# Maxima of a query tile over five even blocks of 462 columns in place of four of 512 and one of 256

## The reference, cut to what matters

```
def layer(x):                      # x: 2 x 48 x 48 x 192
    q, k, v = split_heads(group_norm(x) @ qkv_w + qkv_b)          # 24 x 2304 x 16 each
    attn = (q * 16 ** -0.5) @ k.T + rel_h[..., :, None] + rel_w[..., None, :]   # 2304 x 2304 a head
    attn = softmax(attn, axis=-1)
    return x + join_heads(attn @ v) @ proj_w + proj_b
```

## Time and profile before

| | before |
|---|---|
| median of three runs | 6808.28 us |
| span of the profiled execution | 6801.4 us |
| TensorE busy | 6725.5 us (99%) |
| VectorE busy | 5454.7 us (80%) |
| ScalarE busy | 4753.7 us (70%) |
| max matmuls (L805), 8640 | 3404.1 us, 395 ns each |
| max reductions (L683), 8640 | 5088.7 us, 632 ns each |
| granted clock of TensorE, mean | 0.996 |

### The profile page before, as it was taken

One profiled execution on the slowest core, in us unless ns is written; L12 is line 12 of the kernel. 1 busy time (PEld: TensorE's weight loads), 2 busy tenths in 40 slices (PEclk: granted clock), 3 DMA queues, 4 the chain that ended last, 5 costly groups with the idle time before them and its releaser, 6 DMA issues.

```text
span 6801.4 us, 139326 instructions
## 1 busy us (share of the span) xinstructions
PE 6725.5 (99%) x53600; PEld 4245.8 (62%) x53600; DVE 5454.7 (80%) x9973; ACT 4753.7 (70%) x10225; POOL 938.1 (14%) x967
## 2 busy tenths in 40 slices
PE   7999999999999999999999999999999999999998
PEld 5666666666666666666665666666666666666664
DVE  7887888778887788877888778887888878888883
ACT  3776776767767777677776767767676676767775
POOL 2111010211112110121111210102101121101110
PEclk8999999999999999999999999999999999999999
DMA  6676676767677677667676766767677676777673
GB/s 164 148 156 152 137 160 138 163 151 142 152 144 168 144 143 156 149 158 149 142 155 149 158 143 143 161 145 166 140 144 157 147 165 138 143 152 156 144 154 88
DMA packets 306307, 1013.72 MB, mean 149 GB/s; under 512 B 107440, under 2 KB 196976, under 8 KB 215920
## 3 DMA queue, kind: packets, MB, share of 16 engines
q1 hardware_dynamic: 305648, 1004.81, 68.9%
HBM read 745.26 MB, written 255.69 MB: 147 GB/s over the span
## 4 chain that ended last, share of the span: by engine, by line
PE 96%; DMA 1%; DVE 1%; issue 0%; ACT 0%; SPq 0%; POOL 0%; DVEq 0%; ACTq 0%
PE work L805 30%; PE work L878 27%; PE work L796 27%; PE work L824 7%; PE work L843 3%; PE work L862 2%; PE work L851 1%; DMA moving<-rel_scratch 1%; DVE mpart L683 1%; PE work L830 0%; DVE xb L674 0%; ACT probs L561 0%; DMA back<-attention_scratch 0%; DVE hi L721 0%; PE work L835 0%
## 5 line engine op out<-in xcount | busy, mean ns | idle before, releaser
L683 DVE TENSOR_REDUCE mpart<-work 128x1 f32<-128x512 f32 (+1 forms) x8640 | 5088.7, 632 | 1079.7 <-PE work L805 1013.1
L561 ACT ACTIVATE probs<-work 128x512 f32<-128x512 f32 (+1 forms) x8640 | 4100.2, 564 | 866.6 <-PE work L796 852.1
L805 PE MATMUL work<-mkeys,hi 128*128 128x512 f32 (+1 forms) x8640 | 3404.1, 395 | 10.6 <-DVE mpart L683 8.8
L796 PE MATMUL work<-moving,keys 113*128 113x512 f32 (+1 forms) x8640 | 3299.9, 383 | 10.9 <-DMA moving<-rel_scratch 5.7
L805 PEld LDWEIGHTS work<-mkeys,hi 128*128 128x128 f32 x8640 | 1643.6, 190 | 622.4 <-DVE mpart L683 324.0
L878 PE MATMUL work<-probs,vall 128*17 128x288 f32 x27648 | 2013.1, 409 | 0.0
L796 PEld LDWEIGHTS work<-moving,keys 113*128 113x128 f32 x8640 | 1642.1, 190 | 362.3 <-ACT probs L561 39.2
L878 PEld LDWEIGHTS work<-probs,vall 128*17 128x17 f32 x27648 | 637.3, 96 | 846.8 <-ACT probs L561 358.3
L824 PEld LDWEIGHTS work<-image,tab 128*48 128x48 f32 x6912 | 401.6, 124 | 544.9 <-ACT probs L561 513.2
L490 POOL TENSOR_TENSOR full<-full,hi 128x384 f32<-128x384 f32 x576 | 583.5, 1016 | 938.7 <-DVE hi L721 937.6
L495 POOL TENSOR_TENSOR rden<-oraw,rden 128x576 f32<-128x576 f32 x96 | 137.1, 1428 | 3955.3 <-DMA rden<-inverse_scratch 3955.3
(11 more groups left out here) (42 smaller groups left out, 646.8 us busy)
## 6 DMA issues: line engine op xcount, KB each, us to landing
moving<-rel_scratch SPq DMA_DIRECT2D x1728, 144.0 KB
moving<-qk_scratch SPq DMA_DIRECT2D x288, 576.0 KB
rel_scratch<-hi SPq DMA_DIRECT2D x192, 432.0 KB, 5.7
rel_scratch<-full SPq DMA_DIRECT2D x192, 432.0 KB, 5.5
moving<-rel_scratch SPq DMA_DIRECT2D x288, 288.0 KB
image<-qk_scratch SPq DMA_DIRECT2D x384, 144.0 KB, 3.2
keys<-qk_scratch SPq DMA_DIRECT2D x192, 288.0 KB, 7.8
qk_scratch<-split_hi SPq DMA_DIRECT2D x144, 192.0 KB, 3.9
```

Of the source, the lines that this page charges most:

```text
L561: act.activation(probs[:, tile % RING, lo:up], bank[:, 0:up - lo], ACT.Exp).then_inc(act_read, 1)
L683: dve.tensor_reduce(mpart[:, u % 2, q, m:m + 1], bank[:, 0:MSPLIT[m][1] - MSPLIT[m][0]], AX.X, ALU.max)\
L796: pe.matmul(bank[:, 0:up - lo], tile_of(keys[0:K_ROWS, u % 2, :], c, third), moving[0:K_ROWS, slot_of(u, third)[0], lo:up], start=True, st ...
L805: pe.matmul(bank[:, 0:up - lo], hi[:, u % 2, q * P:(q + 1) * P], mkeys[:, u % 2, lo:up], start=True, stop=True).then_inc(for_dve, 1)
```

## The change

The blocks of the max pass are made even: five of at most 462 columns (462, 462, 462, 462 and 456), from the first column on. The score pass keeps its blocks. Nothing else is edited.

```diff
 SPLIT = [(512 * i, min(512 * i + 512, N)) for i in range(5)]
 SB = len(SPLIT)
-MSPLIT = SPLIT[-1:] + SPLIT[:-1]
+MAX_STEP = 2 * -(-N // (2 * MAXB))
+MSPLIT = [(MAX_STEP * i, min(MAX_STEP * (i + 1), N)) for i in range(MAXB)]
 MT_AT = 2
```

## The result

| | before | after |
|---|---|---|
| median of five runs | 6808.55 us | 6836.32 us (6830.56 to 6841.25) |
| span of the profiled execution | 6801.4 us | 6834.5 us |

The ratio after to before is 1.0041, with a 95% interval of 1.0029 to 1.0053: **slower by 27.8 us**. The forecast was 16.5 us slower, 6825, inside a range of 6806 to 6868. The profiled spans lie further apart, 33.1 us. In every execution of the kernel after, the time is 1.8 us above the span, so the profiled execution of before must have taken about 6803, some 5 us less than its median; the 6.9 us that I put around the span were partly that.

The account below looks back on a forecast made before the run. TensorE was taken to bound the kernel, VectorE counting only where TensorE waits for it. Statistics tiles 9.5, second tiles 6, normalisation 2 and start -1 summed to +16.5 us on 6808.3, so 6825 us, range 6806 to 6868.

Parts of the forecast that it names:

- the 6.9 us that I put around the span: Difference between the profiled span of 6801.4 us and the median of 6808.28, taken as untouched by the change.
- What bounds the kernel: TensorE, busy for 99% of the span; VectorE, busy for 80%, counts only where TensorE waits for an unread bank.
- The line for the max blocks: A 462-column max block costs TensorE 0.211 us, on the line through 256 and 512 columns, 0.457 ns a column.
- The matmuls at 0 a tile: Max matmuls in each tile: first block 0.094 us longer, the four others together 0.094 shorter, sum 0.
- The bound that I gave for a dearer block: Max blocks 2 ns off the line, either way, would be 17 us over 1728 tiles.
- The margin of the ordinary tile: Slack of the fifth max block's weight load behind VectorE's read falls from 0.12 to 0.03 us, still hiding it.
- Statistics tiles +9.5: In 42 tiles with group statistics between the first two reductions, TensorE is held longer, 0.22 us each: +9.5 us.
- Second tiles +6: In about 67 second tiles of units, ScalarE's chain and the last score block's load move by 0.094 us: +6 us.
- Normalisation +2, start -1: Small VectorE steps in the rest of the fourth units: +2 us; tiles ahead of the first scores, banks freed sooner: -1.
- no change that can be measured: Rival, chance 0.33: same mechanism but smaller shifts or a column price under the line, 6806 to 6821 us.
- Cover gone: Rival: every tile's margin falls below zero, 6868 us with 25 ns short; chance 0.14 together with columns not cheaper.
- The short block was costly: Rival, chance 0.07: the 256-column first block is too short to cover a weight load; even blocks save 180 us, 6628.

Follow-up runs that it names:

- short reads: Kernel after the change, with every reduction reading only the first 256 columns of its block: 6795.7 us, ratio 0.9979.
- both moves: On the kernel before: first copy of the attention sums ahead of the bias terms in second tiles, group statistics in slots 3 and 5: 6796.4 us, 0.9983.

## Why the prediction was right, and where not

- **What bounds the kernel**: right. TensorE sets the time, and VectorE counts only where TensorE waits for it: the reductions take as long in sum as before (5447 against 5453 us, "nothing is saved on VectorE"), and the kernel got slower.
- **The line for the max blocks**: right for the block itself. Steps of 0.211 were forecast; the four later blocks of a tile average 211.4 ns (845.8 / 4), 3.8 ns above the line in sum.
- **The matmuls at 0 a tile**: this is the mis-sized term. I priced the blocks that change and took the unchanged score blocks between them to keep their pace; they lost 10 ns a tile. Together with all five max blocks that is 12 ns, 14 us over the 1147 ordinary tiles; with the priced waits taken out of both kernels, 14 us remained by the ratios. The bound that I gave for a dearer block, 2 ns a block or 17 us, was about its size, but it stood for the max blocks, and its reason, the starts, does not explain it alone. That the time still fell inside the range is in part luck: the room above the forecast had been left for other causes.
- **The margin of the ordinary tile**: right. Forecast 0.03, read 0.02, and the load is in time. The short reads show that no hidden wait is left behind it; the kernel with the first block last shows what it costs when it is gone, 10 ns a tile.
- **Statistics tiles +9.5**: +9.5, 226 ns each against 224 (42 of which are 9.4, so the forecast was rounded up). Moving the statistics away took 14.6 us off these tiles, of which 3.6 came back in the tiles behind them.
- **Second tiles +6**: +6.2, 94 ns each against 94, in 66 tiles against 67. Moving the copy removed them.
- **Normalisation +2, start -1**: +2.7, and -2.8 with the end. The estimates were near by luck, for the reasoning was thin: the short reads took 17.6 us off the first place and 11.4 off the second, so VectorE's time weighs more there than I took it to.
- **Not foreseen**: the tiles with the small transpose (t = 14) got 3.6 us shorter. It can't be put down to the change: nine in ten of these tiles differ by less than 25 ns, five that waited long in the profiled execution of before make the sum, and the same tiles have -2.1 us with the blocks of before and both moves and +1.7 with 464 columns. The +2.7 of the tiles with the projection or the values is of that kind too (+5.0 with the blocks of before and both moves).
- **The rivals**: "no change that can be measured" fell with the interval, 1.0029 at the least. "Cover gone" did not happen here. "The short block was costly" fell: 256 at the start of a tile is the cheapest of all first blocks that were tried with the same moves (6796 us, against 6804 with 384, 6805 with 464 and 6814 with 462).

The sum with measured terms: 9.5 + 6.2 + 2.7 - 2.8 + 17.9 + 2.7 - 3.6 + 0.5 = 33.1 between the profiled executions, of which some 5 are the low execution of before; 27.8 between the medians.

## What to carry to other kernels

Even pieces were not better pieces here: in a pipeline whose ring is refilled by reading it out, try to make the piece that starts the chain the small one, and count what stands on its early end. When a tuned kernel gets slower by a few tenths of a per cent, the waits that its trace already shows can be priced from their rows (here 9.5 and 6 us forecast, 9.5 and 6.2 found), and they can also be taken away by moving the work that stands in them, which here gave 12 us on the kernel before. A pace that is the same to 1 ns in two sizes of a block is no promise for a third size, nor for the unchanged block beside it.

## What was not expected of the hardware

Score blocks of 512 columns, alternating with max blocks, take 233 to 235 ns each between max blocks of 512. Between blocks of 462 two of the four take 237 to 238, although nothing in them has changed, nor does the trace show a wait there; between blocks of 464 at multiples of 464 they keep 233 to 236. Starts that are no multiple of 16 columns cost nothing at 512 (0.9998, 0.9989 to 1.0007). But 464 columns at the starts of 462, and 462 columns at the starts of 464, both come out 7 to 8 us above 464 at multiples of 464, once the number of columns is made equal. Neither width nor start explains this by itself, reading VectorE's banks sooner doesn't change it, the clock is the same, and what does cause it stays open.
